# One pass over the attention weights instead of two, and ten gate strips cast to bf16 early, in an eight-core recurrence and MoE block kernel

## The chip, the cores and the metric

The kernel runs on 8 cores of one Trainium2 chip. Each core works on its own 1024 tokens and no core talks to another. The metric is the device time in microseconds of the slowest core, lower is better. The time of the kernel before is 2316.63 us, the median of 2 runs (2311.27 and 2321.99).

## The reference

```python
def _L0_attn_ref(x, W, b):
    lam = jax.nn.sigmoid(jnp.einsum('bkd,ed->bke', x, W) + b)
    def step(s, inp):
        lam_t, u_t = inp
        s = lam_t * s + (1.0 - lam_t) * u_t
        return (s, s)
    s0 = jnp.zeros((x.shape[0], x.shape[2]), dtype=x.dtype)
    _, ys = jax.lax.scan(step, s0, (jnp.moveaxis(lam, 1, 0), jnp.moveaxis(x, 1, 0)))
    return jnp.moveaxis(ys, 0, 1)
...
x = _layernorm(x + _L0_attn_ref(x, W, b), axis=-1)
# ffn: shared = (silu(x sh_gate^T) * (x sh_up^T)) sh_down^T
#      routed = the same with r_gate, r_up, r_down, times a weight of the top 2 of 8 router logits
x = _layernorm(x + shared + routed, axis=-1)
```

x is 4 x 2048 x 2048 in f32. W is 2048 x 2048, sh_gate and sh_up are 8192 x 2048, sh_down is 2048 x 8192, r_gate and r_up are 1024 x 2048, r_down is 2048 x 1024; all of them are f32 in HBM.

## The kernel before

Two cores share a sequence, 1024 tokens each. The recurrence runs along the tokens, so the second core of a pair needs the state at its start. It gets it from a warm-up: each core also loads the 128 tokens ahead of its own (`x_warm`, zeros for the first half) and runs the recurrence over them from zero; the last value of each channel is the initial state (`sinit`).

Every core reads all the weights. A weight is handled in strips of 128 rows by 2048 columns. A strip takes two DMAs: one on GpSimd's queue that reads 1 MB of f32 and writes 0.5 MB of bf16 (called a cast here), and one DMA transpose on SyncE's queue that puts the contraction dimension on the partitions. TensorE then uses the result as its stationary operand, 16 pieces of 128 x 128, against the activations `x_b` (bf16, features on the partitions, 1024 tokens in two halves of 512).

The order of work is the order in which the Python code records it. `P.op` and `P.dma` append to one list, and each engine executes its own instructions of that list in that order, with semaphore waits where a dependency asks for one. A DMA waits on the engine that issues it, and everything recorded behind it for that engine waits too. The queues are ACTQ (ScalarE's), POOLQ (GpSimd's) and SPQ (SyncE's).

The stages, in order:

- **x in.** For the warm tile and for each of the 8 token tiles `tt`: `x_own` is loaded into `xtm` or `xtm2` (L302, 1 MB, ACTQ), transposed by 16 matmuls (L189), copied to `x_fm` by VectorE (L194) and cast to `x_b` by ScalarE (L197). ScalarE issues the next load only after its casts of the tile before.
- **Warm-up pass.** `emit_warmup(k)`, called for k = 0 to 15, two calls after every second tile and the last eight behind the tiles. It streams strip k of `w_attn` (`stream_strip`, cast at L210, transpose at L213) through a ring of two buffers, does 16 matmuls on the 128 warm tokens (L263), a sigmoid (L267), and four small VectorE instructions (L272 to L283) that leave `sinit[:, k]`. Only two ring buffers can be used, since the third lies over `xtm`.
- **Main pass.** A loop over the same 16 strips, which streams each of them a second time, through a ring of three: 32 matmuls on the 1024 tokens (L370), two sigmoids (L377), VectorE's four instructions (L382, L386, the scan L390, L396), and, one strip late, `emit_stats_stage`: a cast and a square on ScalarE (L337, L339) and 4 matmuls that sum them (L346, L351). Behind strips 6, 8, 10, 12 and 14 `emit_ppre` puts 4 casts on POOLQ each that write part of `sh_down` in bf16 to `down_bf` in DRAM (L227).
- **Layer norm 1** and the router.
- **Gate and up.** `gu_strips`, first for the 8 routed strips (stage E0), then for the 64 shared ones (stage E1) in the order 14 to 63, then 0 to 13. For each strip: the cast of the gate rows (L525) and their transpose (L529), the cast of the up rows (L535) and their transpose (L539), then 64 matmuls (L549 for gate, L559 for up), a SiLU (L567) and a product (L574). The rings have two buffers: `wnat` and `wT` for even positions, the four `gub` for odd ones. In E1 one more cast for the down projection follows each strip from number 16 to number 43. At positions 10 and 12 the combine weights of the router go through DRAM (`emit_comb_tail`, `finish_comb`).
- **Down** (L847, L864), whose weights are transposed straight from `down_bf` in DRAM (L832), and **layer norm 2** and the output.

Of the kernel before, what the change touches and what calls it, by code (L numbers as in the profile page):

```python
# [9 lines left out]
BF16 = mybir.dt.bfloat16  # L10
AF = mybir.ActivationFunctionType
# [42 lines left out]
def build_program(stage=None):  # L54
# [20 lines left out]
    down_bf = nc.dram_tensor("down_bf", [D, INTER], BF16).ap()  # L75
    rdown_bf = nc.dram_tensor("rdown_bf", [D, RINTER], BF16).ap()
# [81 lines left out]
    with contextlib.ExitStack() as stk:  # L158
# [41 lines left out]

        wring_nat = [wnat[0], wnat[1], wnat2]
        wring_T = [wT[0], wT[1], wT2]
        wnat_free = [None, None, None]
        wT_free = [None, None, None]
# [24 lines left out]
        def emit_ppre_r(half, quarters=range(4)):  # L229
# [18 lines left out]
        st_scw_arr = [None] * ND  # L248
        st_si_arr = [None] * ND
        st_xw_fm = xw_ev[-1]  # L250
        st_xw_b = xw_cv[-1]

        def emit_warmup(k):
            r = k % 2
            p2 = k % 2
            stT, wTt = stream_strip(w_attn[k * 128:(k + 1) * 128, :], r)
            lam_t, b_t, ys_t = lam[p2], bsc[p2], ysc[p2]
            zw = next_ph()
            mm = None
            for dc in range(ND):  # L260
                lhs = wTt[:, dc * 128:(dc + 1) * 128]
                rhs = xw_b[:, dc * WARM:(dc + 1) * WARM]
                mm = P.op("PE", lambda lhs=lhs, rhs=rhs, zw=zw, dc=dc: nc.tensor.matmul(  # L263
                    PH[zw][:, 0:WARM], lhs, rhs, start=(dc == 0), stop=(dc == ND - 1)),
                    deps=([stT, st_xw_b, ph_free[zw]] if dc == 0 else []),
                    inc=(1 if dc == ND - 1 else 0))
            st_sigw = P.op("ACT", lambda zw=zw, k=k, lam_t=lam_t: nc.scalar.activation(  # L267
                out=lam_t[:, 0:WARM], in_=PH[zw][:, 0:WARM], func=AF.Sigmoid,
                bias=bias_cols[:, k:k + 1], scale=1.0),
                deps=[mm, st_bias, lam_free[p2]])  # L270
            ph_free[zw] = st_sigw
            st_b1 = P.op("DVE", lambda lam_t=lam_t, b_t=b_t: nc.vector.tensor_scalar(  # L272
                out=b_t[:, 0:WARM], in0=lam_t[:, 0:WARM], scalar1=-1.0, scalar2=1.0,
                op0=ALU.mult, op1=ALU.add), deps=[st_sigw, bsc_free[p2]])
            st_b2 = P.op("DVE", lambda b_t=b_t, k=k: nc.vector.tensor_mul(
                b_t[:, 0:WARM], b_t[:, 0:WARM], xw_fm[:, k * WARM:(k + 1) * WARM]),
                deps=[st_b1, st_xw_fm])
            st_scw = P.op("DVE", lambda lam_t=lam_t, b_t=b_t, ys_t=ys_t:
                          nc.vector.tensor_tensor_scan(
                out=ys_t[:, 0:WARM], data0=lam_t[:, 0:WARM], data1=b_t[:, 0:WARM],  # L280
                initial=0.0, op0=ALU.mult, op1=ALU.add),
                deps=[st_b2, ysc_free[p2]])
            st_si = P.op("DVE", lambda ys_t=ys_t, k=k: nc.vector.tensor_copy(  # L283
                sinit[:, k:k + 1], ys_t[:, WARM - 1:WARM]), deps=[st_scw])


            st_scw_arr[k] = st_scw
            st_si_arr[k] = st_si
            lam_free[p2] = st_scw
            bsc_free[p2] = st_scw  # L290
            ysc_free[p2] = st_si
            wT_free[r] = mm

        x_tr_last = xw_tr[-1]
        prev_evac = xw_ev
        prev_read = [xw_tr[-1], None]
        xtms = [xtm, xtm2]
        x_ev_all, x_cv_all = [], []
        for tt in range(NT):
            xt = xtms[tt % 2]  # L300
            src = x_own[tt * 128:(tt + 1) * 128, :]
            stl = P.dma("ACTQ", f"cXTM{tt % 2}", lambda src=src, xt=xt: nc.scalar.dma_start(out=xt[:, :], in_=src),  # L302
                        deps=[prev_read[tt % 2]])
            trs, evs, cvs = tr_in(
                stl, xt,
                lambda dc, tt=tt: x_fm[:, dc * 1024 + tt * 128: dc * 1024 + tt * 128 + 128],
                lambda dc, tt=tt: x_b[:, dc * 1024 + tt * 128: dc * 1024 + tt * 128 + 128],
                extra=[x_tr_last], prev_evs=prev_evac)
# [756 lines left out]
```

How the kernel before makes its waits and increments, by code:

```python
            def emit_for(host):  # L982
                known = {}
                eng = {"PE": nc.tensor, "DVE": nc.vector, "ACT": nc.scalar,
                       "POOL": nc.gpsimd, "SP": nc.sync}[host]
                for (h, fn, deps, inc, sem_name) in P.ops:
                    if h != host:
                        continue
                    for (dn, dv) in deps:
                        if known.get(dn, 0) >= dv:
                            continue
                        eng.wait_ge(sems[dn], dv)
                        known[dn] = dv
                    instr = fn()
                    if inc:
                        instr.then_inc(sems[sem_name], inc)
```

## Time and profile before

| what | value |
| --- | --- |
| median of 2 runs, slowest core | 2316.63 us |
| the profiled execution | 2288.84 us |
| its span (core 0, the slowest) | 2287.3 us |
| spans of all cores | 2238.7 to 2287.3 us |
| TensorE matmul busy | 1770.4 us (77%) |
| VectorE, ScalarE, GpSimd busy | 389.4, 272.7, 132.2 us |
| DMA moved | 352.82 MB, 154 GB/s on average |

The span runs from the first to the last instruction of a core. "DMA share" is the mean busy share of the core's 16 DMA engines; it can pass 1 where packets overlap. "PEclk" is the granted TensorE clock as a share of full speed. The idle time of an engine stands behind `|` or in brackets, with what ended it.

### The profile page before, as it was taken

What the parts mean: (1) busy time and instruction counts of PE and PEld (TensorE: products, weight loads), DVE (VectorE), ACT (ScalarE), POOL (GpSimd) and SP (SyncE); (2) the same over time, 40 slices, a digit from 0 to 9 for tenths busy, and PEclk for the clock granted to TensorE, in tenths of its full rate; (3) what the DMA queues carried; (4) which work ended last, traced back from release to release, by engine and by line L of the source; (5) the groups of instructions that cost most, each with busy time, mean ns of one, the idle gap of its engine ahead of it and who ended that gap; (6) DMA issues with size and microseconds to landing.
All of it is one profiled execution on the core that took longest, in us unless ns stands there. A gap on an engine that the chain in (4) does not pass through costs nothing.

```text
span 2287.3 us, 20924 instructions; the slowest of 8 cores (2238.7 to 2287.3 us)
## 1 busy us (share of the span) xinstructions
PE 1770.4 (77%) x8036; PEld 802.4 (35%) x8036; DVE 389.4 (17%) x656; ACT 272.7 (12%) x472; POOL 132.2 (6%) x253
## 2 busy tenths in 40 slices
PE   2336756158788866866999999979999999999940
PEld 2332222013333322323444444434444444444420
DVE  2323434800012102000000100101000000000032
ACT  2211222210012100000000000000000000000012
POOL 0001111011000100000100000000000000000000
PEclk7557988569899988978999999989999999999975
DMA  6789999499999999999999999999777877787749
GB/s 132 161 157 170 129 150 138 144 155 152 172 122 162 170 120 137 150 109 118 177 158 162 156 150 162 157 126 162 136 177 169 184 165 152 178 184 178 158 103 231
DMA packets 621909, 352.82 MB, mean 154 GB/s; under 512 B 561002, under 2 KB 561131, under 8 KB 619508
## 3 DMA queue, kind: packets, MB, share of 16 engines
q1 hardware_dynamic: 549376, 138.45, 41.7%
q0 software_dynamic: 34848, 130.07, 39.7%
q10 hardware_dynamic: 37588, 82.97, 12.0%
q8 instruction: 66, 1.08, 0.2%
q14 instruction: 31, 0.25, 0.0%
HBM read 313.70 MB, written 67.11 MB: 166 GB/s over the span
## 4 chain that ended last, share of the span: by engine, by line
PE 53%; DMA 24%; SPq 14%; DVE 4%; ACT 2%; issue 2%; ACTq 1%; DVEq 0%; POOL 0%; POOLq 0%
PE PH L847 19%; PE PH L559 14%; PE PH L549 12%; DMA wT<-wnat 10%; SPq L539 9%; DMA gub<-gub 7%; SPq L529 4%; PE PH L370 3%; DMA wnat<-w_attn 3%; DMA xtm<-x_own 2%; PE PH L864 2%; DMA comb_dram<-comb_cols 1%; DMA loT<-r2lo_park 1%; PE PT L189 1%; DVE x_fm L457 1%
## 5 line engine op out<-in xcount | busy, mean ns | idle before, releaser
L549 PE MATMUL PH<-x_b,wT 128*128 128x512 bf16 x1152 | 271.2, 390 | 60.2 <-DMA wT<-wnat 58.4
L559 PE MATMUL PH<-x_b,wT 128*128 128x512 bf16 x1152 | 268.3, 387 | 42.7 <-DMA wT<-wnat 23.2
L559 PE MATMUL PH<-x_b,gub 128*128 128x512 bf16 x1152 | 270.1, 389 | 34.5 <-DMA gub<-gub 34.5
L549 PE MATMUL PH<-x_b,gub 128*128 128x512 bf16 x1152 | 265.5, 384 | 38.1 <-DMA gub<-gub 38.1
L847 PE MATMUL PH<-y_sh,wT 128*128 128x512 bf16 x1024 | 223.8, 379 | 0.9 <-DVE y_sh L574 0.9
L574 DVE TENSOR_TENSOR y_sh<-silu,PH 128x512 bf16<-128x512 f32 x112 | 77.0, 688 | 805.7 <-PE PH L559 775.5
L567 ACT ACTIVATE silu<-PH 128x512 f32<-128x512 f32 x144 | 85.8, 597 | 1023.7 <-PE PH L549 977.7
L549 PEld LDWEIGHTS PH<-x_b,wT 128*128 128x128 bf16 x1152 | 114.6, 100 | 206.4 <-issue 78.6
L559 PEld LDWEIGHTS PH<-x_b,wT 128*128 128x128 bf16 x1152 | 114.1, 99 | 186.2 <-issue 56.5
L559 PEld LDWEIGHTS PH<-x_b,gub 128*128 128x128 bf16 x1152 | 114.5, 100 | 179.5 <-issue 51.1
L549 PEld LDWEIGHTS PH<-x_b,gub 128*128 128x128 bf16 x1152 | 113.6, 99 | 179.1 <-issue 47.2
L847 PE MATMUL PH<-y_sh,wnat 128*128 128x512 bf16 x768 | 171.0, 379 | 0.0
L370 PE MATMUL PH<-x_b,wT 128*128 128x512 bf16 x512 | 126.0, 409 | 32.9 <-DMA wT<-wnat 32.9
L847 PEld LDWEIGHTS PH<-y_sh,wT 128*128 128x128 bf16 x1024 | 99.0, 98 | 124.8 <-issue 7.5
L847 PEld LDWEIGHTS PH<-y_sh,wnat 128*128 128x128 bf16 x768 | 75.1, 98 | 90.6
L874 DVE TENSOR_TENSOR scr<-PH,scr 128x512 f32<-128x512 f32 x32 | 22.1, 691 | 475.3 <-PE PH L864 475.3
L189 PE MATMUL PT<-ident_f,xtm 128*128 128x128 f32 x144 | 32.5, 420 | 89.2 <-DMA xtm<-x_own 65.6
L370 PEld LDWEIGHTS PH<-x_b,wT 128*128 128x128 bf16 x512 | 52.0, 104 | 106.6 <-issue 57.1
L765 ACT CAST r1b_t<-scr 128x1024 bf16<-128x1024 f32 x16 | 16.7, 1045 | 488.4 <-PE PH L847 272.6
L189 PEld LDWEIGHTS PT<-ident_f,xtm 128*128 128x128 f32 x144 | 29.4, 227 | 91.4 <-issue 91.4
L847 PE MATMUL PH<-yback,wnat 128*128 128x512 bf16 x256 | 60.5, 379 | 0.0
L263 PE MATMUL PH<-xw_b,wT 128*128 128x128 bf16 x256 | 24.7, 278 | 32.5 <-DMA wT<-wnat 32.5
(118 smaller groups left out, 826.0 us busy)
## 6 DMA issues: line engine op xcount, KB each, us to landing
down_bf<-sh_down POOLq DMA_DIRECT2D x64, 512.0 KB, 17.0
yback<-ysh_park ACTq DMA_DIRECT2D x128, 256.0 KB, 7.9
wnat<-w_attn POOLq DMA_DIRECT2D x32, 512.0 KB, 8.1
wnat<-sh_gate POOLq DMA_DIRECT2D x32, 512.0 KB, 8.9
wnat<-sh_up POOLq DMA_DIRECT2D x32, 512.0 KB, 8.6
gub<-sh_gate POOLq DMA_DIRECT2D x32, 512.0 KB, 8.4
gub<-sh_up POOLq DMA_DIRECT2D x32, 512.0 KB, 8.5
xtm<-x_own ACTq DMA_DIRECT2D x8, 1024.0 KB, 7.5
```

The lines of the kernel that those rows point to most:

```text
L189: trs.append(P.op("PE", lambda po=po, si=si: nc.tensor.transpose(po, si, ident_f[:, :]), deps=[st_src, st_if] + list(extra) + bank_war))
L263: mm = P.op("PE", lambda lhs=lhs, rhs=rhs, zw=zw, dc=dc: nc.tensor.matmul(PH[zw][:, 0:WARM], lhs, rhs, start=(dc == 0), stop=(dc == ND - 1 ...
L370: mm = P.op("PE", lambda lhs=lhs, rhs=rhs, zi=zi, dc=dc: nc.tensor.matmul(PH[zi][:, :], lhs, rhs, start=(dc == 0), stop=(dc == ND - 1)), d ...
L457: st_h1[k] = P.op("DVE", lambda k=k: nc.vector.tensor_mul(x_fm[:, k * 1024:(k + 1) * 1024], nrm[:, :], rstdB[:, :]), deps=[st_s1, st_rstdB ...
L529: nc.sync.dma_start(out=dstg, in_=natg[:, :], transpose=True),
L539: nc.sync.dma_start(out=dstu, in_=natu[:, :], transpose=True),
L549: nc.tensor.matmul(PH[gi][:, :], lhs, rhs, start=(dc == 0), stop=(dc == ND - 1)),
L559: nc.tensor.matmul(PH[ui][:, :], lhs, rhs, start=(dc == 0), stop=(dc == ND - 1)),
L567: st_s = P.op("ACT", lambda gi=gi, sscr=sscr: nc.scalar.activation(out=sscr[:, :], in_=PH[gi][:, :], func=AF.Silu, scale=1.0), deps=[mmg, ...
L574: nc.vector.tensor_tensor(ydst, sscr[:, :], PH[ui][:, :], op=ALU.mult),
L847: nc.tensor.matmul(PH[pi][:, :], lhs, rhs, start=(q == 0 and c == 0), stop=False),
L864: nc.tensor.matmul(PH[pi][:, :], lhs, rhs, start=False, stop=(c == NR - 1)),
```

## The change

1. The warm-up is no longer a pass of its own. `emit_warmup` is gone, and its instructions stand at the head of each turn of the main loop, on the strip that the turn has streamed anyway. `w_attn` is streamed once, 16 strips and not 32.
2. The tiles of x come first, without warm-up work between them. `wnat_free[2]` and `wT_free[2]`, the third ring buffer, are tied to the last transpose of x from the start.
3. Ten casts are recorded with the tiles of x: rows 14 x 128 to 24 x 128 of `sh_gate` go to `gate_bf` in DRAM. They wait for nothing. In E1 the first ten positions (strips 14 to 23) skip the cast of the gate rows, and their transpose reads `gate_bf` in DRAM.

```diff
+    gate_bf = nc.dram_tensor("gate_bf", [INTER, D], BF16).ap()
...
+        for tt in range(NT):
...
+            gs = 14 + tt
+            gsrc = sh_gate[gs * 128:(gs + 1) * 128, :]
+            gdst = gate_bf[gs * 128:(gs + 1) * 128, :]
+            st_gpre[gs] = P.dma("POOLQ", f"cPG{gs}", lambda gdst=gdst, gsrc=gsrc:
+                                nc.gpsimd.dma_start(out=gdst, in_=gsrc))
+        for gs in range(22, 24):
...
-        wnat_free = [None, None, None]
-        wT_free = [None, None, None]
+        wnat_free = [None, None, x_tr_last]
+        wT_free = [None, None, x_tr_last]
...
-        def emit_warmup(k):
-            r = k % 2
+        for k in range(ND):
+            r = k % 3
             p2 = k % 2
             stT, wTt = stream_strip(w_attn[k * 128:(k + 1) * 128, :], r)
...
-            if tt % 2 == 1:
-                emit_warmup(tt - 1)
-                emit_warmup(tt)
-        for k in range(NT, ND):
-            emit_warmup(k)
...
-        for k in range(ND):
-            r = k % 3
-            p2 = k % 2
-            stT, wTt = stream_strip(w_attn[k * 128:(k + 1) * 128, :], r)
...
-                    deps=[mm, st_scw_arr[k], lam_free[p2]])
+                    deps=[mm, st_scw])
...
-                deps=[st_b2, st_si_arr[k], ysc_free[p2]])
+                deps=[st_b2, st_si])
...
+                if gate_pre is not None and s in gate_pre:
+                    gbs = gate_pre[s][1]
+                    stTg = P.dma("SPQ", f"c{tag}gT{ri}", lambda dstg=dstg, gbs=gbs:
+                                 nc.sync.dma_start(out=dstg, in_=gbs, transpose=True),
+                                 deps=[gate_pre[s][0]] + flat(gTF[ri]))
+                else:
...
+            gate_pre={gs: (st_gpre[gs],
+                           gate_bf[gs * 128:(gs + 1) * 128, :])
+                      for gs in st_gpre})
```

TensorE around the start of the main pass, the kernel before. L189 are the transposes of x, L263 the warm-up matmuls, L370 the main matmuls and L346 and L351 the sums:

```order
L189 MATMUL PT<-ident_f,xtm_92 128x128 x16
L263 MATMUL PH<-xw_b,wT_54 128x128 x16
L263 MATMUL PH<-xw_b,wT_55 128x128 x16
L263 MATMUL PH<-xw_b,wT_54 128x128 x16
L263 MATMUL PH<-xw_b,wT_55 128x128 x16
L263 MATMUL PH<-xw_b,wT_54 128x128 x16
L263 MATMUL PH<-xw_b,wT_55 128x128 x16
L263 MATMUL PH<-xw_b,wT_54 128x128 x16
L263 MATMUL PH<-xw_b,wT_55 128x128 x16
L263 MATMUL PH<-xw_b,wT_54 128x128 x16
L263 MATMUL PH<-xw_b,wT_55 128x128 x16
L370 MATMUL PH<-x_b,wT_54 128x512 x32
```

The same place in the changed kernel, where L190, L326, L356, L304 and L309 are the same operations:

```order
L190 MATMUL PT<-ident_f,xtm_92 128x128 x16
L326 MATMUL PH<-xw_b,wT_54 128x128 x16
L356 MATMUL PH<-x_b,wT_54 128x512 x32
L326 MATMUL PH<-xw_b,wT_55 128x128 x16
L356 MATMUL PH<-x_b,wT_55 128x512 x32
L304 MATMUL PT<-r1b_t,ones_cb 1x512
L309 MATMUL PT<-sqb_t,ones_cb 1x512
L304 MATMUL PT<-r1b_t,ones_cb 1x512
L309 MATMUL PT<-sqb_t,ones_cb 1x512
L326 MATMUL PH<-xw_b,wT_94 128x128 x16
```

The ten groups of warm-up matmuls that stood between the last tile of x and the first main matmul are spread over the main pass, one group ahead of the 32 main matmuls of its strip. So are the three pairs that stood between the tiles.

GpSimd's queue at its start in the changed kernel:

```order
L232 DMA gate_bf<-sh_gate 16x16384 x8
L237 DMA gate_bf<-sh_gate 16x16384 x2
L254 DMA wnat_52<-w_attn 128x2048
L254 DMA wnat_53<-w_attn 128x2048
L254 DMA wnat_93<-w_attn 128x2048
L254 DMA wnat_52<-w_attn 128x2048
```

In the kernel before, the queue begins with the first of 32 loads of `w_attn`; now ten casts of `sh_gate` stand ahead of the first of 16.

SyncE's queue at the end of E0 and the start of E1, before (`wT` and `gub` are the transposed strips, `wnat` and `gub` the natural ones):

```order
L529 DMA_TRANSPOSE gub_69<-gub_68 128x16x128
L539 DMA_TRANSPOSE gub_71<-gub_70 128x16x128
L529 DMA_TRANSPOSE wT_54<-wnat_52 128x16x128
L539 DMA_TRANSPOSE wT_55<-wnat_53 128x16x128
L529 DMA_TRANSPOSE gub_69<-gub_68 128x16x128
```

and in the changed kernel:

```order
L521 DMA_TRANSPOSE gub_69<-gub_68 128x16x128
L531 DMA_TRANSPOSE gub_71<-gub_70 128x16x128
L513 DMA_TRANSPOSE wT_54<-gate_bf 128x16x128
L531 DMA_TRANSPOSE wT_55<-wnat_53 128x16x128
L513 DMA_TRANSPOSE gub_69<-gate_bf 128x16x128
```

The order of the transposes is the same; the gate ones of ten strips read DRAM, and no cast into `wnat` or `gub` stands on GpSimd's queue for them.

## Rows read from the trace of the kernel before

**Rows 1.** Span and mean granted clock of the slowest core
```profile
core 0: 2287.3 us, clock 0.886
```

**Rows 2.** Stretches of core 0: engines' busy time, then PEclk, DMA share, GB/s
```profile
28.00:131.00 103.00, 38.24 (x252) 36.15 (x253) 34.14 (x153) 31.25 (x142) 3.18 (x6) 0.59 0.61 144
131.00:188.00 57.00, 14.59 (x136) 12.55 (x133) 10.93 (x40) 3.83 (x12) 4.77 (x9) 0.54 0.97 168
188.00:392.00 204.00, 143.69 (x572) 56.16 (x572) 85.62 (x63) 50.36 (x62) 24.43 (x46) 0.88 1.02 145
...
609.00:771.00 162.00, 142.91 (x651) 63.42 (x650) 30.51 (x124) 31.96 (x41) 13.77 (x26) 0.96 1.08 148
771.00:1250.00 479.00, 380.60 (x1665) 166.23 (x1664) 47.57 (x78) 33.70 (x55) 39.13 (x74) 0.90 1.12 143
```

**Rows 3.** Groups of TensorE instructions, 131 to 188 us
```profile
L263 PE MATMUL PH<-xw_b,wT 128*128 128x128 bf16 x136 | 14.8, 294 | 32.5 <-DMA wT<-wnat 32.5
```

**Rows 4.** Timeline of TensorE: start, duration, what, idle before
```profile
129.47 1.95 PE L263 MATMUL PH<-xw_b,wT 128*128 128x128 bf16 x32
...
188.71 16.64 PE L370 MATMUL PH<-x_b,wT 128*128 128x512 bf16 x64 [10.62 <-DMA wT<-wnat]
...
231.60 0.38 PE L346 MATMUL PT<-r1b_t,ones_cb 128*1 128x512 bf16 x1 [1.86 <-ACT r1b_t L337]
...
242.25 0.38 PE L346 MATMUL PT<-r1b_t,ones_cb 128*1 128x512 bf16 x1 [1.86 <-ACT r1b_t L337]
...
346.37 9.40 PE L370 MATMUL PH<-x_b,wT 128*128 128x512 bf16 x32 [16.10 <-DMA wT<-wnat]
...
834.36 6.01 PE L559 MATMUL PH<-x_b,wT 128*128 128x512 bf16 x16 [18.08 <-ACT silu L567]
```

**Rows 5.** Groups of TensorE instructions, 188 to 392 us
```profile
L370 PE MATMUL PH<-x_b,wT 128*128 128x512 bf16 x512 | 126.0, 409 | 32.9 <-DMA wT<-wnat 32.9
```

**Rows 6.** The chain that ended last, 0 to 140 us: start, duration, what
```profile
15.35 7.98 DMA xtm<-x_warm
...
28.50 6.49 DMA xtm<-x_own
...
40.09 4.73 DMA xtm<-x_own
...
51.71 7.91 DMA xtm<-x_own
...
126.21 3.43 PE PT L189 x16
```

**Rows 7.** DMA queues, 131 to 188 us: packets, MB, share of 16 engines
```profile
q0 software_dynamic: 1296, 4.72, 51.7%
q1 hardware_dynamic: 19082, 4.81, 45.5%
```

**Rows 8.** DMA queues, 188 to 361 us
```profile
q0 software_dynamic: 4752, 17.30, 72.5%
q1 hardware_dynamic: 30838, 7.77, 30.0%
```

**Rows 9.** DMA queues, 361 to 410 us, twelve casts to `down_bf` alone
```profile
q0 software_dynamic: 1760, 6.33, 96.8%
```

**Rows 10.** DMA queues, 609 to 771 us
```profile
q0 software_dynamic: 3771, 13.69, 59.6%
q1 hardware_dynamic: 40636, 10.25, 48.5%
```

**Rows 11.** Groups of TensorE instructions, 609 to 771 us
```profile
L549 PE MATMUL PH<-x_b,wT 128*128 128x512 bf16 x162 | 38.6, 393 | 12.1 <-DMA wT<-wnat 10.3 <-DVE cntc L626 1.8
L559 PE MATMUL PH<-x_b,gub 128*128 128x512 bf16 x161 | 38.2, 392 | 4.5 <-DMA gub<-gub 4.5
...
L559 PE MATMUL PH<-x_b,wT 128*128 128x512 bf16 x160 | 36.2, 379 | 2.6 <-DMA wT<-wnat 2.6
```

**Rows 12.** The transposes from `down_bf` in DRAM (L832), from issue to landing
```profile
DMA to landing us min/median/max: 4.3/5.7/15.2
```

More of the change, by code:

```diff
@@ L247, in build_program @@
         ysc_free = [None, None]
[L248 to L251, printed above, removed]
-        def emit_warmup(k):
-            r = k % 2
-            p2 = k % 2
-            stT, wTt = stream_strip(w_attn[k * 128:(k + 1) * 128, :], r)
[L257 to L292, printed above, removed]
@@ L361, in build_program @@
             lam_t, b_t, ys_t = lam[p2], bsc[p2], ysc[p2]
+            zw = next_ph()
+            mm = None
+            for dc in range(ND):
+                lhs = wTt[:, dc * 128:(dc + 1) * 128]
+                rhs = xw_b[:, dc * WARM:(dc + 1) * WARM]
+                mm = P.op("PE", lambda lhs=lhs, rhs=rhs, zw=zw, dc=dc: nc.tensor.matmul(
+                    PH[zw][:, 0:WARM], lhs, rhs, start=(dc == 0), stop=(dc == ND - 1)),
+                    deps=([stT, st_xw_b, ph_free[zw]] if dc == 0 else []),
+                    inc=(1 if dc == ND - 1 else 0))
+            st_sigw = P.op("ACT", lambda zw=zw, k=k, lam_t=lam_t: nc.scalar.activation(
+                out=lam_t[:, 0:WARM], in_=PH[zw][:, 0:WARM], func=AF.Sigmoid,
+                bias=bias_cols[:, k:k + 1], scale=1.0),
+                deps=[mm, st_bias, lam_free[p2]])
+            ph_free[zw] = st_sigw
+            st_b1 = P.op("DVE", lambda lam_t=lam_t, b_t=b_t: nc.vector.tensor_scalar(
+                out=b_t[:, 0:WARM], in0=lam_t[:, 0:WARM], scalar1=-1.0, scalar2=1.0,
+                op0=ALU.mult, op1=ALU.add), deps=[st_sigw, bsc_free[p2]])
+            st_b2 = P.op("DVE", lambda b_t=b_t, k=k: nc.vector.tensor_mul(
+                b_t[:, 0:WARM], b_t[:, 0:WARM], xw_fm[:, k * WARM:(k + 1) * WARM]),
+                deps=[st_b1, st_xw_fm])
+            st_scw = P.op("DVE", lambda lam_t=lam_t, b_t=b_t, ys_t=ys_t:
+                          nc.vector.tensor_tensor_scan(
+                out=ys_t[:, 0:WARM], data0=lam_t[:, 0:WARM], data1=b_t[:, 0:WARM],
+                initial=0.0, op0=ALU.mult, op1=ALU.add),
+                deps=[st_b2, ysc_free[p2]])
+            st_si = P.op("DVE", lambda ys_t=ys_t, k=k: nc.vector.tensor_copy(
+                sinit[:, k:k + 1], ys_t[:, WARM - 1:WARM]), deps=[st_scw])
             st_sig = [None, None]
@@ L504, in gu_strips @@
         def gu_strips(wg, wu, nstrips, ydst_fn, scale, scale_dep, ydep_fn,
-                      park_fn=None, order=None, hook=None, rings=None):
+                      park_fn=None, order=None, hook=None, rings=None,
+                      gate_pre=None):
             (gnat, gnatF, gT, gTF, unat, unatF, uT, uTF, tag) = rings
```

89 lines of the change are left out of this document (45 added, 44 removed).

## The prediction

> **What bounds the kernel now.** I read the cores first, then the stretches, then in each stretch the groups, the timeline and the DMA queues. Core 0 is the slowest, with a span of 2287.3 us [rows 1], so its stages set the time. From 28 to 131 us the tiles of x come in, one after the other, with the DMA engines only 0.61 busy. From 131 to 188 us the rest of the warm-up pass runs, and there TensorE works for 14.6 of 57 us while the DMA share is 0.97 [rows 2]; its 32.5 us of waits are all for transposed strips [rows 3]. That stretch is pure weight streaming. From 188 to 392 us the main pass runs with the DMA share at 1.02 and TensorE busy for 143.7 of 204 us [rows 2]. In the first ten strips of E1, about 609 to 771 us, DMA stands at 1.08 and TensorE at 0.88, and from 771 to 1250 us at 1.12 and 0.79 [rows 2]. So from 131 us to 1250 us DMA work is what runs out, with TensorE close behind it. The change takes DMA work out of two of these stretches.
>
> What one transfer occupies on the 16 DMA engines follows from the queue rows. A cast is 0.52 MB, a transpose some 2080 packets. In the warm-up stretch q0 holds 51.7% of 57 us for 9.0 casts, 3.3 us each, and q1 45.5% for 9.2 transposes, 2.8 us each [rows 7]. In the main pass it is 3.8 us for a cast (72.5% of 173 us over 33) and 3.5 for a transpose (30.0% over 14.8) [rows 8]. In early E1 it is 3.7 and 4.0 us [rows 10]. Twelve casts alone take 49 us at 96.8%, 3.9 us each [rows 9].
>
> **The change, part by part.**
>
> *The second pass over w_attn goes.* Between the end of the x transposes (126.21 + 3.43 = 129.6 us, [rows 6]) and the first main matmul (188.71 us, [rows 4]) stands nothing but warm-up work. In the changed kernel strips 0 and 1 are cast and transposed long before that, so the first group of the merged loop starts at about 131 us if x comes in as before. That takes 188.7 - 131 = 58 us off. Strip 2 has to wait for the last x transpose, since its buffer lies over `xtm`. At 3.8 + 3.5 us of engine time and a few of latency it is there about 15 us later, ahead of strip 2's turn at 131 + 2 x 11.7 us. That is covered.
>
> *The warm groups go into the main loop.* A turn of the main loop that waits for no weight takes 242.25 - 231.60 = 10.65 us [rows 4]. To it come 16 matmuls of 128 columns. Two such groups took 1.95 us behind the x transposes [rows 4], so 1.0 us each. In the warm-up stretch, at a granted clock of 0.54, 8.5 groups took 14.6 us, 1.7 us each [rows 2]. I take 1.1 us, since the main loop runs at 0.88 [rows 2]: 16 x 1.1 = 17.6 us, with 16 and 27 us as the ends. The turn is then 11.7 us.
>
> The loop also gains a cross-engine path: sigmoid of the warm group, three VectorE instructions, and only then may ScalarE write the first half of `lam`. VectorE does 85.6 / 16 = 5.4 us a turn now and the small ones add 10.9 / 10 = 1.1; ScalarE has 50.4 / 16 = 3.1 and some 0.4 more [rows 2]. Both are well under 11.7. In the timeline order VectorE is done with strip k some 6 us after the last main matmul of k and with the warm part of k+1 at about 7, while the first half of k+1 leaves TensorE more than 7 us after it (1.9 of wait and the sums [rows 4], 1.1 warm, and half of 126.0 / 16 = 7.9 us [rows 5]). I cost it at nothing; if this thin cover went, it would be a few tenths of a us a turn.
>
> *The waits for strips in the main pass.* Now they are 32.9 - 10.6 (the first one) = 22.3 us [rows 4, 5], the longest of them 16.1 us at 346 us. They come where 4 casts to `down_bf` join two strips: 2 x (3.8 + 3.5) + 4 x 3.8 = 29.8 us of DMA against 2 x 10.65 = 21.3 us of TensorE, a lack of 8.5 us for each of five pairs. With turns of 11.7 the lack is 6.4. Five pairs make 42 us of lack now and 32 after, so up to 10 us less are waited. I take 9 less, with 0 and 15 as the ends.
>
> In a sentence apart: the Trainium skill ("Advanced Engine Details and Errata", X-Bar Transpose) has it that transpose DMAs are as fast as regular ones on this chip. By that a transpose, which moves half of a cast's bytes, would take 1.9 us, a pair 26.6 us against 23.4, and the lack of the five pairs would be 16 us and not 32, so that the 13 us of waits I leave in the loop would mostly go. The trace does not agree, with 2.8 to 4.0 us for each [rows 7, 8, 10].
>
> *The x stage.* Each load waits for ScalarE's casts of the tile before, so the loads stand on the chain. A load takes 4.7 us with the queues empty and 8 us beside casts and transposes [rows 6]. The ten gate casts wait for nothing, are queued at the start and last 10 x 3.9 = 39 us alone [rows 9], with the loads some 50 us. In that time the warm tile and tiles 0 and 1 come in. Shared evenly they would take about 11 us each, where they took 8.0, 6.5 and 4.7: +14 us. Later loads run nearly alone, at 5 to 6 us for 7.9, and the warm groups and sigmoids no longer sit between tiles: about -14 us. I cost the stage at 0. The good end is 8 tiles at the rate of the second one, 11.6 us from issue to issue, which ends the stage at 118 us: -11. The bad end is +18: the first load blocked until the casts are done at about 41 us, where it landed at 23.3.
>
> *E1.* Ten casts leave it. A strip there needs 2 x 3.7 + 2 x 4.0 + 3.7 (down) = 19.1 us of DMA, and TensorE 142.9 us for 643 matmuls [rows 2, 11], 14.2 a strip; without the gate cast it is 15.4. TensorE waits for strips there 10.3 + 4.5 + 2.6 = 17.4 us [rows 11]. I take 12 of them as saved, with 0 and 17 as the ends. The gate transposes read DRAM now. Those of the down projection, which do so too, land in 5.7 us in the median [rows 12], so I cost the new source at nothing. What is late next is the up strip, whose cast and transpose stay. Behind position 10 nothing changes, and with two buffers no lead can be kept. Down, norms and output stay.
>
> The sum: -58 (second pass) + 17.6 (warm groups) - 9 (waits in the loop) + 0 (x stage) - 12 (E1) = -61.4, call it 62 us off. Against the profiled execution of 2288.84 us (span 2287.3 and 1.5 around it) that is 2227 us. The median of the runs, 2316.63, lies 27.8 above that execution; I take the gain off the median: 2254 us. A difference over 2%, 46 us, is about what a measurement of this kernel tells from none; the bound is 2270.
>
> **The rivals.**
>
> 1. *The casts starve the loads of x.* If a cast's big packets go ahead of the loads' as long as any are queued, the x stage takes the bad end, +18. The gain is 62 - 18 = 44 us: 2273 us. For it: loads go from 4.7 to 8 us beside as few as two casts [rows 6]. Against it: the whole backlog is 39 us and half of the stage is behind it. The Trainium skill ("DMA: Bandwidth & Descriptors", Queues, rings and completion order) says that an engine takes turns between queues packet by packet, which would be the even sharing of my forecast; rows 6 agree as far as 8 us against 4.7 goes.
>
> 2. *The relief moves instead of staying.* The waits in the merged loop stay 22 us, as a 4-cast burst holds up one transpose at a time whatever the turn lasts (the 16.1 us are one wait, [rows 4]), and in E1 the next burst takes what the ten strips save. Then it is 58 - 18 = 40 us: 2277 us. For it: most waits are few and long. Against it: the DMA work is really gone in both stretches.
>
> 3. *More than the sum.* The x stage at its good end (11), the whole 17 us in E1, and the 18.1 us wait at 834 us, where ScalarE waits for small DMAs of the combine weights behind casts [rows 4], cut by half (9), and 5 more from the end of E0: 62 + 30 = 92, 2225 us.
>
> 4. *Slower: the gate transposes from DRAM.* Their place is the first ten strips of E1. If one took the engines for as long as the slowest of L832 took to land, 15.2 us [rows 12], a strip would need 3.7 + 3.7 + 4.0 + 15.2 = 26.6 us against 14.2, 124 us of waits where there are 17, and the kernel ends at 2317 - 50 + 107 = 2374 us. It eats the whole gain from 9.5 us a transpose (ten strips of 20.9 - 14.2 wait 67 = 50 + 17). Against it: 64 such transposes pass in the down stage in time, median 5.7 us from issue to landing.
>
> **How the numbers follow.** Forecast 0.55 (2254, its own range 2240 to 2270), rival 1 0.13, rival 2 0.15, rival 3 0.13, rival 4 0.04. Faster by over 2%: nearly all of the forecast (0.53), a quarter of rivals 1 and 2 together (0.07), which stand close to 2270, and rival 3 (0.13): 0.73. Within 2%: 0.23. Slower: 0.04. The range for 8 in 10 reaches down almost to rival 3, and up to where the x stage is at its bad end and E1 gives nothing (62 - 18 - 12 = 32): 2228 to 2286 us.
>
> **What would show it.** Right: first main matmul at 125 to 140 us and not 189; loads of the warm tile and tiles 0 and 1 at 9 to 12 us, the later ones near 5; turns of 11.7 us in the first six strips; waits for strips in the loop of 10 to 18 us; the first sums of the norm some 50 us earlier than 392; waits for strips of at most 8 us in the first ten strips of E1, and landings of the `gate_bf` transposes of 4 to 9 us. Wrong: an x stage that ends beyond 150 us (rival 1), waits in the loop over 25 us or longer waits behind position 10 than before (rival 2), turns much over 12 us where no strip is late (the cross-engine path), or `gate_bf` transposes over 9 us with TensorE waiting for them (rival 4).

## The result and the profile after

The changed kernel takes 2238.11 us (median of 11 runs). The kernel before, run on the same chip, takes 2308.31 us (median of 10). The ratio is 0.968, with a 95% interval of 0.964 to 0.972, so the change is faster by 3.2%, some 70 to 75 us. Forecast were 2254 us and 62 us. Some executions of most kernels are slow ones (up to 2491 us here), nearly always at a lower granted clock; the ratios leave them out, the medians do not.

The profiled execution took 2247.7 us. Span and granted clock of its cores:

```profile
core 0: 2184.4 us, clock 0.914
...
core 3: 2246.2 us, clock 0.904
...
core 5: 2211.7 us, clock 0.906
```

The slowest core is now number 3, and it is an outlier, so one profile's slowest core against another's [rows 1] says little: 2287.3 - 2246.2 = 41 us. I therefore take, for each kernel, the mean over its eight cores of the time at which a stage begins. I read it off each core's TensorE records (first x transpose, first main matmul, first gate matmul, and so on). That mean of the spans falls by 58 us, from 2263.0 to 2204.9, and the stages add up to it (the first row is a part of the second):

| stage, mean over the cores, us | before | after | difference | forecast |
| --- | --- | --- | --- | --- |
| first x transpose | 23.1 | 67.3 | +44.2 | |
| start of the kernel to the last x transpose | 133.1 | 150.9 | +17.8 | 0 (-11 to +18) |
| from there to the first main matmul | 58.6 | 2.1 | -56.5 | -58 |
| main loop | 192.0 | 203.5 | +11.5 | +8.6 |
| layer norm 1, E0 | 257.8 | 256.8 | -1.0 | 0 |
| E1, first ten strips | 163.3 | 144.8 | -18.5 | -12 |
| E1, the next 53 strips | 835.4 | 825.2 | -10.2 | 0 |
| last strip, down, norm 2, output | 622.9 | 621.6 | -1.3 | 0 |

**The x stage.** It answers to [rows 6]. These are pieces of the chain that ended last on core 3, from 0 to 160 us (start, duration, what). "ACTq L181" is ScalarE's sequencer issuing the loads of the attention bias, 16 DMAs of 128 elements that stand ahead of `x_warm` on its queue:

```profile
3.40 1.13 ACTq L181
...
9.72 9.81 ACTq L181
19.56 19.55 ACTq L181
39.14 12.17 ACTq L181
51.34 3.10 ACTq L181
...
59.79 7.52 DMA xtm<-x_warm
...
72.54 6.07 DMA xtm<-x_own
...
83.64 5.03 DMA xtm<-x_own
...
94.00 4.82 DMA xtm<-x_own
...
148.96 3.66 PE PT L190 x16
```

Before, the load of `x_warm` was issued at 15.35 us and took 7.98 [rows 6]. Now it is issued at 59.79 and takes 7.52. The load was not slow; the instruction that starts it came 44 us late, because single bias loads, 0.5 KB each, held ScalarE's queue for 10 to 20 us. Behind that, tiles come every 10.1 us where they came every 13.4 (means over the cores), and 8 x 3.3 = 26 us of the 44 come back, so the stage ends only 18 us late.

The DMA queues of that core from 20 to 50 us, in which nothing is under way but gate casts and bias loads. First come the packets of all queues with the number of small ones, then each queue's packets, MB and share of 16 engines; q10 carries the loads of ScalarE's queue:

```profile
DMA packets 394, 3.28 MB, mean 109 GB/s; under 512 B 294, under 2 KB 294, under 8 KB 294
...
q0 software_dynamic: 197, 3.28, 96.0%
q10 hardware_dynamic: 197, 0.00, 0.6%
```

The two queues stand at 197 packets to 197, one for one. Of the cast queue's packets 97 are among the 294 small ones and 100 carry the data, so one of those holds 3.28 MB / 100 = 33 KB and occupies its engine for 30 us x 16 x 0.96 / 100 = 4.6 us. On the other queue a data packet is a single bias element. A bias load has 128 of them, 8 on each engine, and every one waits for its turn. In [rows 9], where casts write rows of `down_bf`, a packet holds 3.6 KB on the mean. The Trainium skill ("DMA: Bandwidth & Descriptors", Queues, rings and completion order) has it that an engine takes turns between queues a packet at a time, and the counts agree with that. I had quoted this rule for the loads of x and not thought of what 2048 one-element packets do under it, nor of how large a packet of these casts is.

**The main loop and E1.** Stretches, first of core 3, then of core 0 (columns as in [rows 2]):

```profile
1.50:60.00 58.50, 0.00 (x0) 0.00 (x0) 0.00 (x0) 0.00 (x0) 6.07 (x12) 1.00 0.99 111
60.00:152.00 92.00, 31.91 (x143) 29.25 (x144) 29.29 (x137) 30.20 (x136) 0.00 (x0) 0.69 0.36 113
152.00:366.00 214.00, 160.68 (x827) 76.84 (x825) 100.84 (x133) 56.64 (x87) 24.86 (x47) 0.88 1.02 136
```

```profile
595.70:734.00 138.30, 138.30 (x643) 62.68 (x642) 31.08 (x132) 34.82 (x44) 11.05 (x21) 1.00 0.90 157
```

For 58 us TensorE, VectorE and ScalarE are idle, and the DMA engines are at 0.99 with the casts; then DMA stands at 0.36 while x comes in. So the change moved ten casts into a stretch in which the DMA engines were 0.61 busy [rows 2], but packed them at its front. In the first ten strips of E1 (the line from 595.70 us), core 0 has TensorE busy for all of 138.3 us and DMA at 0.90. What it has to be held against is not the stretch from 609 to 771 us in [rows 2, 11], as the prediction has it. E1 begins at 637.0 us on that core, so that stretch is the last two strips of E0 and the first eight of E1. The first ten strips of E1, kernel before, core 0:

```profile
637.00:805.80 168.80, 145.26 (x642) 63.77 (x642) 31.06 (x132) 34.82 (x44) 15.89 (x30) 0.94 1.11 151
```

So 168.8 us became 138.3 on this core: TensorE's idle time went from 23.5 us to nothing, and its busy time fell by 7.0. Two of the groups of TensorE instructions in the changed kernel:

```profile
L541 PE MATMUL PH<-x_b,wT 128*128 128x512 bf16 x161 | 36.6, 379 | 0.0
L551 PE MATMUL PH<-x_b,wT 128*128 128x512 bf16 x160 | 36.2, 379 | 0.0
```

No wait is left, and the matmuls run at 379 ns on the mean (granted clock 1.00, that is 2.4 GHz, over a stretch without a wait) where the gate matmuls from `wT` took 393 with waits of 12.1 us ahead of them and a clock of 0.94 in the stretch. The warm groups in the loop of core 3, which answer to [rows 5]:

```profile
L356 PE MATMUL PH<-x_b,wT 128*128 128x512 bf16 x512 | 121.2, 398 | 0.0
L326 PE MATMUL PH<-xw_b,wT 128*128 128x128 bf16 x256 | 24.7, 273 | 17.3 <-DMA wT<-wnat 17.3
```

Since the warm group now heads each turn, the waits for a strip stand with it. The waits are 17.3 us on core 3 and 0.1 on core 0.

### The profile page after: what moved, and what is told of

Same layout as the page of the kernel before. It is cut to its first block, busy times and chain, and to the rows that moved or that the text cites. A ratio compares the mean times of both kernels' runs of the same rounds, so it can differ in the third digit from the quotient of the medians.

```text
span 2246.2 us, 20803 instructions; the slowest of 8 cores (2184.4 to 2246.2 us)
## 1 busy us (share of the span) xinstructions
PE 1756.3 (78%) x8036; PEld 799.8 (36%) x8036; DVE 388.5 (17%) x656; ACT 272.7 (12%) x472; POOL 122.8 (5%) x237
## 4 chain that ended last, share of the span: by engine, by line
PE 64%; DMA 18%; SPq 7%; DVE 4%; ACTq 3%; ACT 2%; issue 1%; DVEq 0%; POOL 0%; POOLq 0%
PE PH L842 20%; PE PH L551 18%; PE PH L541 17%; DMA gub<-gub 6%; DMA wT<-wnat 4%; SPq L531 4%; PE PH L356 3%; SPq L521 2%; ACTq L181 2%; PE PH L859 2%; DMA gub<-gate_bf 2%; DMA xtm<-x_own 2%; DMA comb_dram<-comb_cols 1%; DMA loT<-r2lo_park 1%; DVE x_fm L442 1%
## 5 line engine op out<-in xcount | busy, mean ns | idle before, releaser
L551 PE MATMUL PH<-x_b,gub 128*128 128x512 bf16 x1152 | 267.5, 386 | 45.7 <-DMA gub<-gub 45.7
L551 PE MATMUL PH<-x_b,wT 128*128 128x512 bf16 x1152 | 266.4, 385 | 42.0 <-ACT silu L559 22.4
L541 PE MATMUL PH<-x_b,wT 128*128 128x512 bf16 x1152 | 264.9, 384 | 21.5 <-DMA wT<-wnat 21.5
L190 PE MATMUL PT<-ident_f,xtm 128*128 128x128 f32 x144 | 32.5, 420 | 120.1 <-DMA xtm<-x_warm 67.5
L356 PE MATMUL PH<-x_b,wT 128*128 128x512 bf16 x512 | 121.2, 398 | 0.0
L356 PEld LDWEIGHTS PH<-x_b,wT 128*128 128x128 bf16 x512 | 52.0, 103 | 62.8 <-issue 10.9
L190 PEld LDWEIGHTS PT<-ident_f,xtm 128*128 128x128 f32 x144 | 29.5, 227 | 122.7 <-issue 122.7
L566 DVE TENSOR_TENSOR y_r<-silu,PH 128x512 bf16<-128x512 f32 x16 | 11.0, 688 | 206.6 <-PE PH L551 200.4
```

The lines of the kernel that those rows point to most:

```text
L190: trs.append(P.op("PE", lambda po=po, si=si: nc.tensor.transpose(po, si, ident_f[:, :]), deps=[st_src, st_if] + list(extra) + bank_war))
L356: mm = P.op("PE", lambda lhs=lhs, rhs=rhs, zi=zi, dc=dc: nc.tensor.matmul(PH[zi][:, :], lhs, rhs, start=(dc == 0), stop=(dc == ND - 1)), d ...
L541: nc.tensor.matmul(PH[gi][:, :], lhs, rhs, start=(dc == 0), stop=(dc == ND - 1)),
L551: nc.tensor.matmul(PH[ui][:, :], lhs, rhs, start=(dc == 0), stop=(dc == ND - 1)),
L566: nc.vector.tensor_tensor(ydst, sscr[:, :], PH[ui][:, :], op=ALU.mult),
```

## The experiments

The first question was which half of the change carries the gain, the single pass or the early gate casts; the second, what it is in the casts that delays the x stage; the third, where the DMA work that bounds E1 can go instead. The theories stand in the expectations, as put down before each run. The table holds what the ten experiments gave, beside the two kernels, stages as above (mean over cores, us); their edits follow. At a threshold of 2%, `rows` and `best` are unclear, `gate_only` is the same as before, and all others are faster.

| kernel | ratio to before (95%) | median us | x in ends | main loop | E1, first ten | mean span |
| --- | --- | --- | --- | --- | --- | --- |
| before | 1 | | 133.1 | 192.0 | 163.3 | 2263.0 |
| after | 0.968 (0.964 to 0.972) | 2238.11 | 150.9 | 203.5 | 144.8 | 2204.9 |
| single_pass | 0.956 (0.949 to 0.962) | 2208.64 | 106.4 | 208.8 | 172.3 | 2190.2 |
| gate_only | 1.006 (1.002 to 1.010) | 2323.55 | 179.9 | 193.1 | 148.7 | 2279.4 |
| bias_late | 0.966 (0.958 to 0.974) | 2229.67 | 144.4 | 205.8 | 146.6 | 2191.1 |
| paced | 0.959 (0.951 to 0.967) | 2226.50 | 123.4 | 206.0 | 144.0 | 2180.9 |
| rows | 0.978 (0.968 to 0.988) | 2254.84 | 153.7 | 204.7 | 148.8 | 2208.7 |
| rows_bias | 0.965 (0.958 to 0.973) | 2214.90 | 137.3 | 205.3 | 143.5 | 2185.3 |
| single_bias | 0.966 (0.957 to 0.976) | 2226.24 | 100.1 | 199.7 | 173.9 | 2178.7 |
| best | 0.971 (0.958 to 0.984) | 2228.71 | 124.7 | 203.3 | 149.9 | 2169.5 |
| prefetch | 0.939 (0.932 to 0.947) | 2187.87 | 61.4 | 199.4 | 164.0 | 2131.5 |
| down_late | 0.912 (0.906 to 0.919) | 2100.95 | 62.0 | 205.9 | 140.7 | 2062.3 |

The kernel before, run beside them, had medians of 2329.84 us (single_pass to paced), 2303.38 (rows to best) and 2307.61 (the last two). Ratios compare better than medians.

### One half of the change at a time

`single_pass` is the changed kernel without the gate casts:

```diff
-            st_gpre[gs] = P.dma("POOLQ", f"cPG{gs}", ...)     # all ten
...
-            gate_pre={gs: (st_gpre[gs], ...) for gs in st_gpre}  # now empty
```

> The changed kernel without the ten gate casts at the start; E1 casts all its gate strips into SBUF as before. Queue theory (the casts at the start held up ScalarE's sixteen small bias loads, and with them the first load of x, by 44 us): the warm tile is issued at about 15 us, tiles follow at 10 us each, the x stage ends near 110 us and not at 151, the first ten strips of E1 take about 163 us and not 145. Net 42 - 18 = 24 us below the changed kernel, about 2214 us. Rival (the casts at the start are hidden, the late start has another cause): the x stage still ends near 150 us and only the 18 us in E1 come back, about 2256 us.

`gate_only` is the kernel before, with two passes, and with the ten gate casts at its start and the gate transposes from DRAM:

```diff
+        for gs in range(14, 24):
...
+            st_gpre[gs] = P.dma("POOLQ", f"cPG{gs}", lambda gdst=gdst, gsrc=gsrc:
+                                nc.gpsimd.dma_start(out=gdst, in_=gsrc))
```

> The kernel before with only the ten gate casts at the start and their transposes from DRAM; the two passes over the attention weights stay. Queue theory: the warm tile is issued at about 60 us and not 15, the end of the x stage moves from 133 to 165 to 175 us, the warm-up pass behind it stays, E1 gains 18 us: 15 to 25 us slower than before, about 2328 us. Rival (the E1 part is a gain by itself): 12 to 18 us faster than before, about 2293 us.

Without the gate casts the x stage ends at 106.4 us, 27 earlier than before the change and 44.5 earlier than with them, and E1's first ten strips take 172.3 us, 27.5 more than with them. The load of `x_warm` in `single_pass`, on the chain of core 1, with the next two tiles:

```profile
15.22 7.17 DMA xtm<-x_warm
...
27.64 4.85 DMA xtm<-x_own
...
37.58 4.76 DMA xtm<-x_own
```

It is issued at 15.22 us as in [rows 6], and tiles follow at 10 us. So the 27 us are what the x stage gains when no warm-up pass runs between the tiles. Most of it is in the loads: the eight on the chain took 7.1 us each on the mean in the kernel before (core 0) and take 4.8 here, 8 x 2.3 = 18 us. I had named this good end and put it at 11 us. The casts alone on the kernel before give 14.6 us in E1 (163.3 to 148.7) and take 47 in the x stage (133.1 to 179.9): 1.006, slower by what can just be told. (The mean span is only 16 us longer. The other 16 came back in stages whose work did not change, which is the size by which executions of equal work differ, as said at the end.) So the gain of the change is the single pass, and the gate casts as placed give nothing. `single_pass` is even ahead of the full change, 0.956 to 0.968, though a variant of it below is not.

### Where the 44 us in the x stage come from

`bias_late` moves the 16 bias loads behind the loads of tiles 4 to 7, four behind each, and `paced` ties the gate casts to the tiles of x:

```diff
+            if tt >= 4:
+                st_bias = load_bias(range(4 * (tt - 4), 4 * (tt - 3)))
```

```diff
+            for gs in ((14, 15), (16, 17), (18, 19), (20, 21), (22,), (23,), (), ())[tt]:
...
+                                    nc.gpsimd.dma_start(out=gdst, in_=gsrc), deps=[stl])
```

> The changed kernel with the sixteen bias loads moved from ahead of the warm tile to tiles 4 to 7, four each; the ten gate casts stay at the start. Even sharing between the queues: the warm tile is issued at about 4 us and lands within 12 us, tiles 0 to 2 take about 8 to 11 us each, the x stage ends near 110 us, 2200 us in all. Rival (a load is held up until the casts are gone): the warm tile or tile 0 lands only past 40 us, the x stage ends near 130 us, about 2217 us. If neither the small loads nor the order matter: 2238 us.

> The changed kernel with the gate casts tied to the tiles of x: two each wait for the load of tiles 0 to 3, one each for tiles 4 and 5; the bias loads stay where they are. Queue theory: the small loads are quick again, the warm tile is issued at about 15 us, tiles take 10 to 12 us, the x stage ends at 115 to 120 us and E1 keeps its gain: about 2204 us. Rival (DMA work moved into the x stage costs as much as it gives wherever it stands): 2230 to 2240 us.

Both missed. For `bias_late` I had expected the x stage to end near 110 us, or 130 by the rival, and it ended at 144.4; for `paced` 115 to 120, and it was 123.4. With the bias loads out of the way `x_warm` is issued at 3.4 us, and still TensorE gets it at 57.3. The tile `xtm` of core 2 in `bias_late`, its load and what that took from issue to landing:

```profile
L207 ACTq DMA_DIRECT2D xtm<-x_warm x1: 1113/1113/1113, 3.4 to 3.4; - x1
...
DMA to landing us min/median/max: 53.7/53.7/53.7
```

So the bias loads were only the first in line. A load of 1 MB that took 7.2 us in `single_pass` takes 53.7 beside the backlog. The queues of that core, from 3 to 30 us and then from 30 to 57, show that this has two halves:

```profile
q0 software_dynamic: 175, 3.11, 106.8%
q10 hardware_dynamic: 292, 0.01, 0.9%
...
q0 software_dynamic: 198, 2.32, 74.3%
q10 hardware_dynamic: 160, 1.05, 14.8%
```

In the first half ScalarE's queue moves 0.01 MB, and the 1.05 MB of the load all go in the second. Ahead of `x_warm` there still stand the loads of the other constants, two of them ([128, 1] columns, `ones_cb` and `eps_c`) in 128 single elements each. In the trace's packet records the first 8 KB packet of `x_warm` starts at 32.2 us on this core, and at 30.5 to 33.2 on the eight cores. So some 29 us went by behind two tiny loads, and 25 in the load's own 128 packets, 8 on each engine, beside the casts'. While they pass, from 32 to 56 us, the queues again stand one for one, at 157 packets to 157, and in that half the casts move 2.2 bytes for each byte of x. That is rival 1's state, reached not because the casts go ahead, but because their packets are longer. No run moves these two constant loads as well. `paced` confirms the place of the casts as the cause: with at most two beside a tile the stage ends at 123.4 us, 27 earlier than in the changed kernel, and E1 keeps its gain (144.0). It is still 17 us later than without casts.

### The size of the packets

`rows` gives the DRAM tile twice the pitch, so that a cast writes 128 rows of 2048 and no longer one contiguous block; `rows_bias` adds the late bias loads.

```diff
-    gate_bf = nc.dram_tensor("gate_bf", [INTER, D], BF16).ap()
+    gate_bf = nc.dram_tensor("gate_bf", [INTER, 2 * D], BF16).ap()
...
-            gdst = gate_bf[gs * 128:(gs + 1) * 128, :]
+            gdst = gate_bf[gs * 128:(gs + 1) * 128, 0:D]
```

> The changed kernel with one difference: gate_bf has twice the row pitch, so that each gate cast goes as 128 rows of 2048 and not as 16 runs of 16384 elements. Packet theory (the queues take turns packet by packet, and a packet of the contiguous casts holds an engine for 3 us where one of a row cast holds it for 0.4): the bias loads take about a us each, the warm tile is issued near 20 us and lands in 8 to 15 us, the x stage ends at 112 to 122 us and not at 151, about 2205 us in all. Rival (a load is held up by any backlog of casts, whatever their packets): the warm tile is issued only near 60 us again, 2238 us.

> The same, and the bias loads moved behind the loads of tiles 4 to 7. Packet theory: the warm tile is issued at 3.4 us and lands by 15 us and not at 57, the first three tiles take 8 to 10 us each to land, the x stage ends at 100 to 110 us, about 2195 us. Rival: the warm tile lands past 40 us as with the contiguous casts, 2230 us.

The queues of core 6 in `rows`, 20 to 57 us:

```profile
DMA packets 2132, 3.90 MB, mean 105 GB/s; under 512 B 1181, under 2 KB 1181, under 8 KB 2132
...
q0 software_dynamic: 1066, 3.90, 95.3%
q10 hardware_dynamic: 1066, 0.00, 33.4%
```

The casts' data packets are now 951 of 4.1 KB, 0.59 us each (37 x 16 x 0.953 / 951), and the two queues stand at 1066 to 1066, one for one. Yet the x stage did not move (153.7 us); here I was wrong. The 16 bias loads make 2048 one-element packets, 128 on each engine. Twelve casts in rows make 12 x 128 / 16 = 96 data packets on each. With contiguous gate casts it is 26, 10 of 33 KB and 16 of 4 KB for the two `w_attn` strips. In either form the tiny packets outlast the casts', so the bias loads are held nearly as long as there are casts. The packet records agree: once the casts run out, 1649 packets of ScalarE's queue pass from 57 to 60 us in the changed kernel, and 1080 from 62 to 70 us in `rows` (128 of them `x_warm`). With the bias loads late the packet size does count. The chain of core 6 in `rows_bias`:

```profile
3.35 22.61 DMA xtm<-x_warm
...
31.00 15.55 DMA xtm<-x_own
...
51.65 16.58 DMA xtm<-x_own
...
73.54 7.41 DMA xtm<-x_own
```

`x_warm` lands in 22.6 us and not in 53.7 (its first packet starts at 17.0 us, again behind the two constant loads), and then the next two tiles pay, 16 us each. The stage ends at 137.3 us against 144.4, where 100 to 110 was expected.

### Are the gate casts worth having at all?

`single_bias` is `single_pass` with the late bias loads. `best` adds to it what should have been the best of all: strips 0 and 1 cast first, then nine row-wise gate casts, one behind the warm tile and each of tiles 0 to 6, and one more.

```diff
+        pre = [stream_strip(w_attn[k * 128:(k + 1) * 128, :], k) for k in range(2)]
...
+        emit_gpre(14, st_xw_l)
...
+            if tt < 7:
+                emit_gpre(15 + tt, stl)
+        emit_gpre(22, None)
```

> The changed kernel without any gate cast at the start (E1 casts its gate strips as before) and with the bias loads behind the loads of tiles 4 to 7. The warm tile is issued at 3.4 us and not at 15, everything behind it comes 11 us earlier than without the gate casts alone: x stage ends near 95 us, ratio 0.951 where that one has 0.956. Rival: the 11 us are lost again in the DMA-bound stages behind, 0.956.

> Row casts, one each behind the landing of the warm tile and of tiles 0 to 6 and a ninth at the end (nine strips and not ten), the first two attention strips ahead of them, the bias loads behind tiles 4 to 7. Each cast is 4 us of DMA in a tile of 10 us. The x stage ends at 95 to 102 us and the first nine strips of E1 run without waits, about 20 us off E1: ratio 0.943, some 2175 us. Rival (casts in the x stage cost there what they give in E1): 0.951 as without them.

The expectations were missed by both, single_bias with 0.966 for 0.951 and best with 0.971 for 0.943. In the stages, nine casts cost 24.6 us in the x stage (100.1 to 124.7) and give 24.0 in E1 (173.9 to 149.9). So even one at a time a cast costs there what it gives here. (The mean span of `best` is 9 us shorter, its ratio no better; I count that as no difference.) An x load is on the chain in that stage, and most of those beside a cast took 7 to 8 us where they take 4.8. `single_bias` lies at 2178.7 on the mean of the cores, 11 ahead of `single_pass`, but behind it in the median of its runs; the two intervals overlap, and I make nothing of that difference.

### Taking the x loads off the chain, and the casts to where DMA is idle

`prefetch` is `single_bias` with each tile of x loaded one tile ahead, into the other of the two buffers:

```diff
+        st_xl = {0: load_x(0, None)}
...
-            stl = P.dma("ACTQ", f"cXTM{tt % 2}", ..., deps=[prev_read[tt % 2]])
+            stl = st_xl[tt]
+            if tt + 1 < NT:
+                st_xl[tt + 1] = load_x(tt + 1, prev_read[(tt + 1) % 2])
```

`down_late` adds to it that the first 20 of the 28 casts for the down projection in E1 (behind strips 16 to 35) are issued in the first ten turns of the down stage:

```diff
-            if 16 <= s < 16 + len(ppre_pieces):
+            if 36 <= s < 16 + len(ppre_pieces):
...
+            if k < 10:
+                for i in (2 * k, 2 * k + 1):
+                    emit_ppre(11 + i // 4, quarters=[i % 4], deps=[st_r2h[1]])
```

> The changed kernel without gate casts, bias loads behind tiles 4 to 7, and each tile of x loaded one tile ahead (ScalarE issues the load of tile tt+1 before the casts of tile tt, tile 0 goes to the second buffer at once). A tile then takes some 5 us and not 10: the x stage ends at 55 to 65 us where it ends at 100 without this, the first main matmul follows at once, and everything behind comes some 38 us earlier: ratio 0.940. Rival (the stages behind are bound by DMA work that only moves): less than 10 us of it stays, 0.955 to 0.96.

> The same, and the twenty casts to down_bf that follow strips 16 to 35 in E1 moved into the first ten turns of the down stage, two a turn, where the DMA share is 0.76. If the waits of E1 are there because a cast too many stands in each strip (19 us of DMA against 14.2 of TensorE, 15.4 without), the first 22 strips lose most of their waits, 60 to 80 us, and the down stage, at 0.76 + 2 x 3.8 / 32 = 1.0 in ten turns, gives back at most 20: 45 us below the kernel before it in this list, ratio 0.92. Rival (the same casts cost the down stage what they cost E1): within 10 us of it.

Both came out near what was expected, 0.939 and 0.912. With loads ahead the x stage ends at 61.4 us, 39 earlier than in `single_bias`. E1 is the clearest case in the study. The stretch of its first 30 strips and that of the first strips of the down stage, in `prefetch` on core 3:

```profile
514.60:1075.20 560.60, 447.40 (x1929) 194.04 (x1926) 69.86 (x190) 58.50 (x84) 46.88 (x89) 0.89 1.14 145
1531.00:1700.00 169.00, 168.06 (x776) 75.11 (x775) 10.99 (x14) 9.21 (x10) 0.00 (x0) 1.00 0.83 179
```

and in `down_late` on core 4:

```profile
536.00:985.10 449.10, 424.09 (x1926) 189.73 (x1926) 69.67 (x190) 58.50 (x84) 35.27 (x67) 0.97 1.02 152
1442.80:1612.00 169.20, 168.26 (x778) 75.23 (x777) 10.99 (x14) 9.20 (x10) 4.12 (x8) 1.00 0.97 200
```

In the first stretch DMA falls from 1.14 to 1.02, and TensorE's busy share rises from 0.80 to 0.94. In the second the DMA share rises from 0.83 to 0.97 and TensorE stays busy for 168 us of 169. On the mean of the cores the 30 strips take 451 us where they took 532, while the tail moves by -1.3 us. The twenty casts were on the path in E1, and lie beside TensorE in the down stage. `down_late` beats both kernels, by 8.8% and, by the two ratios, by about 5.8% (0.912 / 0.968 = 0.942).

## Why the prediction was right, and where it was not

The sum came out nearer than its terms. The terms that were priced (second pass, x stage, main loop, E1's first ten strips) were to give -61.4 us and gave -56.5 + 17.8 + 11.5 - 18.5 = -45.7. The other -12.5 of the 58 us on the mean of the cores stand in stages that were to give nothing, and I know no cause for them. That part of the agreement is luck.

**The second pass.** Forecast -58, measured -56.5. The first main matmul follows the last x transpose at once, as strips 0 and 1 were there. The step is right. Where it said "131" the run says 153.0 us on the mean, because the x stage ended late; that is the next term.

**The x stage.** Forecast 0, measured +17.8, at the bad end of its range. This is the term that failed. "Shared evenly they would take about 11 us each" assumed that sharing is by bytes or time. The queues went packet for packet (197 to 197, 1066 to 1066), and a data packet of these casts held 33 KB and its engine for 4.6 us. I had also counted the loads of x alone on ScalarE's queue and not the 16 constant loads ahead of them, which were the first thing to be held. The bad end was priced for the right kind of event, "the first load blocked until the casts are done", but put that at 41 us. It was 60 us, as two casts of `w_attn` stand in the same backlog and a cast took 4.6 us there and not 3.9 (from 3 to 57 us the cast queue moved 5.97 MB, which is 11.4 casts, at 96.9% of the engines: 54 x 0.969 / 11.4). The size of the loss, 18 us, agreed by luck: the first load landed not 18 but 44 us late, and 26 us of that came back because the tiles then came at 10.1 us, which was better than I had used. Of the signs named ahead, "an x stage that ends beyond 150 us" came true (150.9), and "loads of the warm tile and tiles 0 and 1 at 9 to 12 us" did not, with 7.5, 6.1 and 5.0 on core 3: by then the casts were done. For this term rival 1 is thus right in place and size, and wrong in the rule it gave; its total, 2273 us, was 35 too high.

**The warm groups and the waits in the loop.** Forecast +17.6 - 9 = +8.6, measured +11.5. A group took 24.7 / 16 = 1.54 us and not 1.1, so the groups cost 24.7 us, within the ends of 16 and 27. Part came back: the main matmuls took 121.2 us and not 126.0 [rows 5]. A turn without a wait is (203.5 - 9.7) / 16 = 12.1 us on the mean, for a forecast of 11.7. Waits for strips in the loop are 9.7 us on the mean where 13 were forecast. The two longest on core 3, to be held against the 16.1 us in [rows 4], come at strip 4, ahead of the casts to `down_bf`, and in the midst of them:

```profile
205.99 1.86 PE L326 MATMUL PH<-xw_b,wT 128*128 128x128 bf16 x16 [8.10 <-DMA wT<-wnat]
...
317.07 1.87 PE L326 MATMUL PH<-xw_b,wT 128*128 128x128 bf16 x16 [9.23 <-DMA wT<-wnat]
```

The path over ScalarE and VectorE costs nothing that shows: the wait ahead of the first sum is 1.86 us a turn, as in [rows 4].

**E1.** Forecast -12, measured -18.5 in this pair. I had taken 12 of 17.4 us of waits and nothing from the clock, and had read the waits in the wrong stretch, as said above. On core 0 the first ten strips of E1 had 23.5 us of idle time. All of it went, and TensorE's busy time fell by 7.0 us as well. Seven kernels with the early gate casts have 143.5 to 149.9 us there (gate_only included), and the four with neither those nor the late down casts have 163.3 to 173.9. So the gain of the casts in E1 is real, 15 to 28 us by which two kernels one compares. The gate transposes from DRAM land in 6.3 and 7.7 us (medians on core 0) and 8.1 and 10.0 (core 3), mostly within the 4 to 9 forecast. In the first ten strips of E1, core 3 alone waits for one of them, 23.8 of the 31.6 us by which it is slower there than core 0:

```profile
L541 PE MATMUL PH<-x_b,gub 128*128 128x512 bf16 x160 | 38.3, 395 | 23.8 <-DMA gub<-gate_bf 23.8
```

One transpose in 80 was waited for. It was issued at 767 us and took 40.7 us to land, but that is not rival 4, for the source in DRAM was not what was slow. The casts issued on that core beside it, which do not touch `gate_bf`, took 32 to 36 us, and from 765 to 808 us its DMA engines were at 1.22 and moved 77 GB/s, where they moved 139 at 0.91 from 654 to 765 us:

```profile
wnat<-sh_up POOLq DMA_DIRECT2D x1, 512.0 KB, 32.2
down_bf<-sh_down POOLq DMA_DIRECT2D x1, 512.0 KB, 34.3
gub<-sh_gate POOLq DMA_DIRECT2D x1, 512.0 KB, 36.4
gub<-gate_bf SPq DMA_TRANSPOSE x1, 40.7
```

What slowed them all I did not find out.

**The rest.** The 10 us less in the strips of E1 behind the tenth are not explained by any term. Kernels with the same work there differ as much from one execution to the next (from the 14th strip to the 31st: 281.6 to 304.8 us), so I do not count them as an effect. Nor do I know why the medians differ by 70 us and the means of the profiled cores by 58.

**As a whole.** The time came out 16 us below the forecast, 8 of them because the kernel before has a median of 2308.31 us by now and not 2316.63. The mechanism that carries it, one pass for two, is confirmed by `single_pass`. The second half of the change, which I had credited with 12 us for nothing, brings nothing net: 15 to 28 us in E1 for 44 in the x stage, of which 5 came back in the loop. The range had one slip: 2317 - 32 is 2285, where it says 2286.

## What to carry to other kernels

Work moved into a stretch with idle DMA engines is only free if no load there is on the chain. Ask for each such load how many packets of the moved transfers it will stand behind and how long one of them holds an engine, and count the tiny loads of constants on its queue too. Move bulk transfers to a stretch in which the compute engine is busy throughout (here the down stage, DMA 0.83), and where loads are on the chain, first take them off it by loading one tile ahead. And test the halves of a change apart: here one of the two carried all the gain.

## What was not expected of the hardware

- The shape of a DRAM-to-DRAM cast went with the size of its packets: the contiguous 128 x 2048 block went in data packets of 33 KB, 4.6 us each, and the same block with a row pitch in packets of 4.1 KB, 0.59 us each.
- With both queues backed up they advanced packet for packet whatever the sizes: 197 to 197 in 30 us with 33 KB beside single elements, 1066 to 1066 in 37 us with 4.1 KB beside single elements, 157 to 157 in 24 us with 33 KB beside 8 KB.
- A DMA of 0.5 KB in 128 single elements held the engine that issues it for up to 19.6 us when the 16 engines were full of such casts. A 1 MB load behind two DMAs of single elements landed after 53.7 us and not 7.2, and about half of that passed before its first packet.
- The time booked on a one-element packet is not fixed. In `rows` 1066 of ScalarE's packets took 33.4% of the 16 engines for 37 us, 0.19 us each; in the changed kernel 197 took 0.6% for 30 us, 0.015 each. Why, no run shows.
